# Attention and quantized feed-forward on one core: the weighted sums of a group as one burst of 32 products instead of two of 16

## The reference

```python
x = L0_attn_x                      # (16, 512, 128)
xn = _layernorm(x, axis=-1)
x = x + _L0_attn_ref(xn, ...) + _L0_ffn_ref(xn, ...)

# attention: 16 query heads of 8 features, 4 key/value heads, causal
q = _rope((xn @ Wqa @ Wqb).reshape(b, s, 16, 8))
k, v = ...                         # (b, s, 4, 8), each repeated for 4 query heads
scores = einsum('bqhd,bkhd->bhqk', q, k) * D ** -0.5, masked above the diagonal
out = einsum('bhqk,bkhd->bqhd', softmax(scores), v) @ Wout + bout

# feed-forward, 352 hidden features; fp4_linear quantizes both operands in blocks of 16
h = silu(fp4_linear(x, w_gate)) * fp4_linear(x, w_up)
return fp4_linear(h, w_down)
```

## Time and profile before

| | us |
|---|---|
| median of 3 runs | 797.62 (795.21 to 798.21) |
| the profiled execution's own time | 797.94 |
| its span in the trace | 795.9 |
| PE busy | 722.8 (91%) |
| DVE busy | 644.0 (81%) |
| POOL busy | 612.3 (77%) |
| ACT busy | 535.1 (67%) |

### The profile page before, as it was taken

The page is one execution under the profiler, slowest core; times in us unless marked ns, Lnnn a source line. Parts: engine busy times, 40 slices in busy tenths (PEclk is TensorE's granted clock), DMA queues, the critical chain, the costliest instruction groups (busy, mean ns, idle before and its releaser), DMA issues.

```text
span 795.9 us, 18365 instructions
## 1 busy us (share of the span) xinstructions
PE 722.8 (91%) x6453; PEld 442.3 (56%) x6453; DVE 644.0 (81%) x1390; ACT 535.1 (67%) x1154; POOL 612.3 (77%) x708
## 2 busy tenths in 40 slices
PE   2467889999999999999999999999999999998986
PEld 1233455665656565665656565565656665665434
DVE  6569788989888888989888988889888988878412
ACT  2213686867777777777776767777776867676672
POOL 5534597878889797878889797878889797856662
PEclk9998899999999999999999999999999999999998
DMA  4423233233334343243334343343434333341111
GB/s 113 115 68 88 73 86 102 86 108 110 96 92 116 104 118 96 89 117 98 103 99 119 88 116 96 91 115 96 108 99 116 87 117 93 93 102 38 56 49 35
DMA packets 85028, 75.48 MB, mean 95 GB/s; under 512 B 28642, under 2 KB 67010, under 8 KB 84938
## 3 DMA queue, kind: packets, MB, share of 16 engines
q1 hardware_dynamic: 84938, 74.32, 34.3%
HBM read 40.45 MB, written 27.25 MB: 85 GB/s over the span
## 4 chain that ended last, share of the span: by engine, by line
PE 39%; POOL 32%; ACT 11%; DVE 7%; issue 6%; DMA 3%; SPq 2%; POOLq 0%; DVEq 0%; ACTq 0%
PE pv_ps L1160 10%; POOL P L554 9%; PE exp_ps L1139 7%; POOL h L564 5%; PE max_ps L1124 5%; ACT P L961 5%; POOL h L567 5%; POOL h L570 4%; PE misc_ps L1184 3%; PE max_ps L1125 3%; PE misc_ps L1192 3%; DVE neg_max L737 3%; PE misc_ps L1209 3%; POOL q_split L645 2%; POOL rstd L596 2%
## 5 line engine op out<-in xcount | busy, mean ns | idle before, releaser
L737 DVE TENSOR_REDUCE neg_max<-max_ps 128x1 f32<-128x512 f32 (+3 forms) x768 | 429.9, 593 | 87.1 <-PE max_ps L1125 85.2
L961 ACT ACTIVATE P<-exp_ps 128x512 f32<-128x512 f32 x512 | 294.9, 599 | 167.7 <-PE exp_ps L1139 166.6
L1139 PE MATMUL exp_ps<-Q,K 128*128 128x512 bf16 (+3 forms) x1024 | 244.0, 301 | 10.3 <-ACT P L961 6.5
L1124 PE MATMUL max_ps<-K,Q 128*128 128x384 bf16 (+2 forms) x768 | 199.2, 278 | 18.9 <-DMA Kd<-K 11.7
L1125 PE MATMUL max_ps<-Kd,Q 128*128 128x128 bf16 x1024 | 191.3, 221 | 2.1 <-DVE neg_max L737 2.0
L554 POOL TENSOR_SCALAR_AFFINE_SELECT P<-P 128x512 f32<-128x512 f32 x256 | 161.8, 667 | 26.8 <-ACT P L964 26.8
L1160 PE MATMUL pv_ps<-P,V 128*32 128x512 f32 (+3 forms) x2048 | 163.9, 438 | 1.9 <-POOL P L554 0.8
L1124 PEld LDWEIGHTS max_ps<-K,Q 128*128 128x128 bf16 x768 | 75.9, 100 | 93.3 <-DVE neg_max L737 47.2
L1125 PEld LDWEIGHTS max_ps<-Kd,Q 128*128 128x128 bf16 x1024 | 98.4, 100 | 46.1 <-issue 22.7
L1139 PEld LDWEIGHTS exp_ps<-Q,K 128*128 128x128 bf16 x1024 | 79.7, 98 | 48.4 <-ACT P L961 27.1
L585 POOL TENSOR_TENSOR h<-gate_sb,up_half 128x352 f32<-128x352 f32 x64 | 59.6, 932 | 58.7 <-DVE gate_sb L750 58.6
(11 more groups left out here) (128 smaller groups left out, 974.1 us busy)
## 6 DMA issues: line engine op xcount, KB each, us to landing
Q<-q_scr SPq DMA_DIRECT2D x64, 224.0 KB
o_scr<-oT SPq DMA_DIRECT2D x31, 256.0 KB, 2.6
q_scr<-q_split SPq DMA_DIRECT2D x16, 384.0 KB, 2.6
Kd<-K SPq DMA_DIRECT2D x64, 96.0 KB
x_in<-x SPq DMA_DIRECT2D x16, 256.0 KB, 4.5
q_scr<-q_split SPq DMA_DIRECT2D x16, 256.0 KB, 2.9
x_res<-x SPq DMA_DIRECT2D x16, 256.0 KB, 5.7
out<-y SPq DMA_DIRECT2D x32, 128.0 KB, 4.3
```

The lines of the kernel that those rows point to most:

```text
L737: nc.vector.tensor_reduce(neg_max[:, pr // 4, heads[0]:heads[0] + len(heads), pr % 4, i], max_ps[r % 3][:, 0:len(heads) * n].rearrange("p ...
L961: nc.scalar.activation(P[g % 2][:, hh + r % 2, col:col + 512], ps[:, :], ACT.Exp, scale=SCALE).then_inc(exp_done, 1)
L1124: nc.tensor.matmul(ps[:, col:col + d], Qt, Kt[:, half, g, 0:d], start=True, stop=True)
L1139: last = nc.tensor.matmul(exp_ps[n % 2][:, col:col + width], K[par][:, half, pr // 2, kb * 128:(kb + 1) * 128], Q[par][:, pr, kb * 128:S], ...
```

## The change

The function `weighted_sums` loses its argument `second`. It is called at the end of odd slots only, waits there for everything that the two halves waited for (the exponentials, all four maskings, `oT_done` for even groups, `v_ready` for group 0), and then issues all four blocks of keys in the order 0, 3, 1, 2.

```diff
-            def weighted_sums(T, off, g, second):
+            def weighted_sums(T, off, g):
 
                 if not T.has(off):
                     return
-                if not second:
-                    T.wait(pe, exp_done, NPAIR * NEXP, off, 2 * NEXP * (g + 1))
-                    T.wait(pe, causal_done, NT * KVH, off, NT * g + 2)
-
-                    if g % 2 == 0:
-                        T.wait(pe, oT_done, 2, off, g // 2)
-                    if g == 0:
-                        T.wait(pe, v_ready, 2, off, 2)
-                else:
-                    T.wait(pe, causal_done, NT * KVH, off, NT * (g + 1))
-                for kb in PV_BLOCKS[second]:
+                T.wait(pe, exp_done, NPAIR * NEXP, off, 2 * NEXP * (g + 1))
+                T.wait(pe, causal_done, NT * KVH, off, NT * (g + 1))
+
+                if g % 2 == 0:
+                    T.wait(pe, oT_done, 2, off, g // 2)
+                if g == 0:
+                    T.wait(pe, v_ready, 2, off, 2)
+                for kb in PV_BLOCKS[0] + PV_BLOCKS[1]:
...
-                if second:
-                    last.then_inc(pv_done, 1)
+                last.then_inc(pv_done, 1)
...
-                    weighted_sums(T, -1 if slot < 2 else 0, (slot // 2 + 3) % 4, slot % 2 == 1)
+                    if slot % 2 == 1:
+                        weighted_sums(T, -1 if slot < 2 else 0, (slot // 2 + 3) % 4)
```

## The result

The changed kernel takes 845.88 us (median of 4 runs, 845.37 to 847.35) against 796.41 us for the kernel before on the same chip: ratio 1.063, 95% interval 1.060 to 1.065. It is 49 us slower; 821 us (807 to 831) was forecast. The direction was right, the size was off by half of the loss.

The account below looks back on a forecast made before the run. It took TensorE and VectorE waiting for each other in turn as the bound. Pair changes 1.08 + 0.41 - 0.13 + 0.28 = 1.64 us, times 14 = 23.0 us, plus 1 for the first and last batch, gave 821 us, range 807 to 831.

Parts of the forecast that it names:

- they add: Step on all slot pairs: each starts with VectorE and ScalarE idle, so one pair's loss isn't made good by the next.
- What the burst costs: Step on the weighted sums: merged burst 2.30 us, 1.08 us more than a half; merging alone saves 0.13 us per group.
- Change +1.08 us: Term for slots 4/5: VectorE never waits for TensorE there, so burst B starts no earlier and the pair lengthens by 1.08 us.
- burst A: First half of a group's weighted sums, in the even slot; the change removes it there, for at most 1.21 us.
- no new wait: Claim that the maskings, the copy of `pv_ps` and the exponentials burst A waited for have a whole slot more.
- Slots 6/7, g = 0.67: Term: without burst A, burst B begins 0.67 us earlier, counted from the pair's start; pair change +0.41 us.
- burst B: Second half of a group's weighted sums, at the odd slot's end; as the merged burst it grows by 1.08 us.
- Slots 0/1, g = 1.21: Term: tiles and projection can come earlier, so burst B moves up the full 1.21 us; pair change -0.13 us.
- Slots 2/3, g = 0.8: Term: VectorE is the limit, so burst B moves up only 0.8 us; pair change +0.28 us.
- The signs of failure: Forecast fails if `onT` comes earlier in its pair, burst B of slots 0/1 doesn't move up, or TensorE's clock falls.
- The two with no loss: Whole-kernel rivals: only the merging counts, 790 us, chance 0.04; the loss is hidden, within 4 us of 798, chance 0.06.
- g is 0 in every pair: Rival: burst B starts no earlier in any pair, 60 us lost, 858 us; cases between 831 and 858, chance 0.10.

## Why the prediction was wrong, step by step

- **What bounds the kernel: right in part.** The time is made of waits between TensorE and VectorE. But "they add" is wrong: a pair's loss shifts GpSimd against the next pair. With group 1 alone merged, slots 4/5 lose 1.08 us and slots 6/7 gain 0.57; with group 0 alone, slots 2/3 lose 0.54 us and slots 4/5 lose 1.73 at full clock.
- **What the burst costs: right.** The merged burst takes 2.29 us from its start to the next tile (436.67 to 438.96), forecast 2.30.
- **Slots 4/5, "Change +1.08 us": this step failed.** It measured +2.80. The 1.08 us for the burst is shown by the run with group 1 alone (+1.08). The rest is the length of `onT`, which I took from its row as a fixed 1.32 us. That length was itself a wait: `onT` needs 0.68 us, and had 0.64 us of waiting for L585 in it. Behind L564 it became 2.94 us, +1.62 us, and it starts 0.10 us later in the pair: 1.08 + 1.62 + 0.10 = 2.80.
- **"Its work doesn't hang on burst A", of GpSimd: wrong.** It hangs on it one pair earlier, by the exponentials and casts of slot 3. I had followed GpSimd only in slots 6/7 and only as something that TensorE waits for, and had written "no new wait" after going through the semaphores. This wait has no semaphore. The run with group 0 alone shows the way: slots 2/3 changed, slots 4/5 lengthened.
- **Slots 6/7, g = 0.67: wrong in sign.** The pair is 0.31 us shorter than before. I took VectorE's queue for the limit. But from the first product of h to burst B TensorE takes 2.89 us in both kernels, and that product starts 1.38 us earlier in the pair, 5.48 us after its start instead of 6.86. First the kernel before, then after:

```profile
433.54 0.63 PE L1209 MATMUL misc_ps<-ident,h 128*128 128x128 f32 x4 [0.26 <-POOL h L570]
```

```profile
458.68 0.60 PE L1205 MATMUL misc_ps<-ident,h 128*128 128x128 f32 x4
```

  Burst A no longer stands ahead of it, and the wait for GpSimd's h is gone (one of 1.3 us is left of the 13), because in the longer slots 4/5 GpSimd gets ahead. When GpSimd is held back for `onT`, the wait is there again (15 times, 6.0 us), the product starts after 5.99 us, and the pair takes 11.18 us, +0.21 over the kernel before. That `x_scale` takes 0.17 instead of 0.79 us, since the bias addition no longer stands beside it, is worth 0.14 us of a pair by itself, as the two runs with the bias later show.
- **Slots 0/1, g = 1.21: measured 0.69.** My walk let VectorE's `q_cos` follow at once and overlooked that the up product of slot 1 waits for it, since it uses the same bank: 1.3 us of that wait in all before, 8.5 us after.
- **Slots 2/3, g = 0.8: measured 0.54.** The mechanism was wrong too: by the rows the limit is ScalarE, which I had left out of this pair, not VectorE. The last exp tile of slot 3 starts 0.05 us after ScalarE's exponential two tiles before has ended, in the kernel before (413.24 and 413.19) as after (435.89 and 435.84), and burst B follows it by 0.78 us in both.
- **The sum.** With the exclusion taken out (GpSimd waits for `onT`) the iteration takes 46.04 us against the forecast 46.0, and the kernel 821.6 us against 821. That the sum fits so well is partly luck: with `onT` at 0.68 us slots 4/5 and 6/7 are 0.53 and 0.20 us below my terms, and 0/1 and 2/3 are 0.77 us above theirs.
- **The signs of failure.** They looked at where `onT` starts, and it starts as forecast; what changed is that it ends 1.7 us later.
- **The rivals.** The two with no loss are out, and 846 us lies in the band between 831 and 858 us. But it isn't that rival, in which g is 0 in every pair: it was 0.54, 0.69 and 1.39 us in three of them, and far below 0 (-1.72) in slots 4/5.

The Trainium skill (SBUF — State Buffer, Who interferes with whom) states the rule that I didn't weigh: a VectorE instruction with two SBUF inputs contends with a GpSimd instruction that reads SBUF, the port pair is an exclusive lock, and "Issue order, not op shape, decides who blocks." All of it agrees with these runs: 1.32, 2.94 and 0.68 us for the same `onT`, by what GpSimd had under way when it was issued, and 3.31 instead of 2.86 us for L564 where `onT` came first. It should have been one of the rivals: `onT` stood 0.7 us ahead of a 2.9 us step of GpSimd, in an edit that moves things by 1.2 us. Its price could be worked out from the old trace: `onT` ended 0.55 us after L585 there, and GpSimd's additions of this size take 2.9 us, so up to 2.9 + 0.55 - 1.32 = 2.1 us for each iteration, 30 us in all. The old trace even held the collision itself. In the last two of the 14 iterations GpSimd has no statistics to compute and reaches L564 early; `onT` takes 2.11 and 2.04 us there, and slots 4/5 of the first of them 12.24 us instead of 11.44. VectorE, then GpSimd, in the kernel before:

```profile
688.79 2.11 DVE L779 TENSOR_TENSOR onT<-o_raw,o_spread 128x512 f32<-128x512 f32 x1
```

```profile
687.50 2.85 POOL L564 TENSOR_TENSOR h<-h,h_mag 128x1408 f32<-128x1408 f32 x1
```

Again `onT` ends 0.55 us after L564 (690.35). I had taken one iteration for all 14.

## What to carry to other kernels

When an edit moves work between engines by some time d, look at each VectorE step on the critical chain that works from SBUF to SBUF, those with two operands above all, and at what GpSimd starts within d of it: a change of their order can cost up to the length of GpSimd's step (here 1.62 us for a step of 2.86), and no semaphore shows it. A duration in a profile can hold a wait; compare the same form elsewhere before it goes into a sum as fixed (the `onT` of the last batch, on 64 partitions instead of 128, takes 0.68 us, most others 1.32, those of the last two of the 14 iterations 2.11 and 2.04), and go through all iterations, the odd ones at the end too. And a burst that lies where its engine would have waited anyway is free, whatever the engine's busy share says: before work is gathered into one burst, count how much of it such places hide.

## What the runs showed of the hardware

- **The clock falls after a pause of TensorE, but not after each.** Behind a stretch of 2.1 us with 0.30 us of TensorE work the granted clock was 0.59 in one iteration of a run (all groups but one merged) and 1.00 in another of the same run, seven like the first and five like the second. A stretch of 2.5 us with 0.82 us of work was followed by 3.2 us at 0.50 (`onT` early). In the changed kernel a stretch of 2.40 us with 0.33 us of work was followed by full clock; of its 14 iterations only the first has the lower clock in slots 4/5 (15.84 us instead of 14.23). What makes the difference stays open. It matters for reading such experiments: the same 24 products and their neighbours take 2.5 or 4.1 us.
- **A tiny step can be held up as well.** `x_scale` reads and writes 32 elements for each partition. It took 0.79 us beside GpSimd's addition, 0.17 us without it.
